# Node MLP on one NeuronCore: edge means transposed in two stacked copies of 64 rows, and their product with the first layer's edge weights made from rounded parts

## What is computed

```
sums   = segment_sum(edge_attr, src)              # 100000 x 64 -> 6250 x 64
counts = segment_sum(ones, src)
edge_attr_agg = sums / max(counts, 1)             # the edge means
combined = concat([layernorm(x), edge_attr_agg, u[batch]], axis=1)   # 256 + 64 + 128 columns
h = relu(combined @ W1 + b1)                      # 512 hidden values
x = x + (h @ W2 + b2)                             # back to 256
```

## Time and profile before

| | us |
|---|---|
| median of 3 runs | 3084.15 (3078.67 to 3087.76) |
| the profiled execution, its own time | 3059.02 |
| span of its instructions | 3056.9 |
| the node MLP, from the last bucket sum to the last T1 | about 1298 to 1484 |
| PE busy in the whole span | 2239.9 (73%) |
| DVE busy | 1911.5 (63%) |
| POOL busy | 2051.8 (67%) |

### The profile page before, as it was taken

The page is one execution under the profiler, slowest core; times in us unless marked ns, Lnnn a source line. Parts: engine busy times, 40 slices in busy tenths (PEclk is TensorE's granted clock), DMA queues, the critical chain, the costliest instruction groups (busy, mean ns, idle before and its releaser), DMA issues.

```text
span 3056.9 us, 49337 instructions
## 1 busy us (share of the span) xinstructions
PE 2239.9 (73%) x14353; PEld 2057.8 (67%) x14354; DVE 1911.5 (63%) x2802; ACT 931.3 (30%) x2542; POOL 2051.8 (67%) x1683
## 2 busy tenths in 40 slices
PE   0000037768999978899699994878888777899897
PEld 0000026658888878877599994766667667899897
DVE  8879986733333222256487767965654555599897
ACT  0000002220111110023466662444544422355453
POOL 5777877777777777201166664787877831588886
PEclk9999998885555555589899997998988885799999
DMA  6543245454444434122112124777777765022231
GB/s 207 152 123 95 77 114 150 144 159 129 126 113 114 119 96 131 60 68 75 41 41 60 50 61 142 196 192 187 197 194 186 195 203 126 25 82 72 64 92 33
DMA packets 342896, 358.31 MB, mean 117 GB/s; under 512 B 210796, under 2 KB 250076, under 8 KB 342513
## 3 DMA queue, kind: packets, MB, share of 16 engines
q1 hardware_dynamic: 210925, 196.63, 22.6%
q0 software_dynamic: 105984, 93.52, 13.5%
q10 hardware_dynamic: 25853, 66.46, 7.0%
HBM read 234.79 MB, written 122.74 MB: 117 GB/s over the span
## 4 chain that ended last, share of the span: by engine, by line
PE 44%; POOL 23%; issue 13%; DVE 13%; DMA 5%; SPq 2%; ACT 1%; DVEq 0%; POOLq 0%; ACTq 0%
POOL sorted L1042 17%; PE ps L2011 13%; POOL mid L1118 5%; PE ps L2060 3%; PE ps L2160 3%; PE ps L2179 2%; PE ps L2038 2%; PE ps L2115 2%; PE ps L2117 2%; PE ps L2116 2%; PE ps L2137 1%; PE ps L2138 1%; PE ps L2136 1%; DVE hT L1650 1%; PE ps L2170 1%
## 5 line engine op out<-in xcount | busy, mean ns | idle before, releaser
L2011 PE MATMUL ps<-big 128*128 128x65 f32 x2380 | 528.1, 420 | 86.7 <-issue 52.5
L2011 PEld LDWEIGHTS ps<-big 128*128 128x128 f32 x2380 | 514.1, 332 | 102.0 <-issue 100.9
L1118 POOL DMA_INDIRECT mid<-h_rows,idx_a x400 | 484.4, 1211 | 131.9 <-issue 115.4
L1415 DVE TENSOR_TENSOR big<-ps,big 128x1792 f32<-128x1792 f32 x85 | 171.6, 2020 | 204.9 <-PE ps L2011 163.3
L1042 POOL DMA_INDIRECT sorted<-yb,idx_a x200 | 239.3, 1196 | 83.9 <-issue 60.0
L1051 POOL TENSOR_TENSOR rstd<-var,neg_half 125x2 f32<-125x2 f32 (+1 forms) x75 | 64.2, 856 | 326.3 <-DVE var L1470 326.1
L1042 POOL DMA_INDIRECT sorted<-xh,idx_b x200 | 237.4, 1187 | 61.0 <-issue 60.3
L1042 POOL DMA_INDIRECT sorted<-mid,idx_b x200 | 237.3, 1187 | 60.9 <-issue 60.3
L1042 POOL DMA_INDIRECT sorted<-wk,idx_a x200 | 237.3, 1187 | 61.0 <-issue 60.3
L2160 PE MATMUL ps<-mid 125*128 125x96 f32 x1600 | 219.8, 300 | 72.2 <-issue 25.1
L2160 PEld LDWEIGHTS ps<-mid 125*128 125x128 f32 x1600 | 211.2, 213 | 84.5 <-issue 57.4
(11 more groups left out here) (336 smaller groups left out, 6307.5 us busy)
## 6 DMA issues: line engine op xcount, KB each, us to landing
h_in_r<-h_parts SPq DMA_DIRECT2D x245, 256.0 KB, 4.4
big<-sorted ACTq DMA_DIRECT2D x85, 469.0 KB, 4.1
sorted<-hT SPq DMA_DIRECT2D x73, 469.0 KB, 7.3
mid<-in_L_ffn_w SPq DMA_DIRECT2D x16, 1024.0 KB
hid_x<-hT ACTq DMA_DIRECT2D x25, 500.0 KB, 4.1
mid<-hid_x SPq DMA_DIRECT2D x25, 500.0 KB
h_parts<-h_part_r SPq DMA_DIRECT2D x25, 480.0 KB
mid<-h_rows,idx_a POOLq DMA_INDIRECT x400
```

Source lines behind the costliest of these rows:

```text
L1118: nc.gpsimd.indirect_dma_start(mg4[:, s, i, :], None, h_rows, bass.IndirectOffsetOnAxis(idx4[:, s, i:i + 1], 0)).then_inc(s_gk[s], 16)
L1415: v.tensor_tensor(node_hot[:, s % 2], lo_near.unsqueeze(1).to_broadcast([BR, GA, BR]), rows2[:, s, :, CW:CW + 1].to_broadcast([BR, GA, BR] ...
L2011: i_ = mm(banks[:, bass.ds(o_, CW)], node_hot[:, s % 2, i, :], rows2[:, s, i, 0:CW], start=False, stop=True, skip_group_check=True)
```

## The change

`agg` becomes `agg2`, two copies of the 64 columns side by side per node, in `big` instead of `mid`: DVE writes the means to the first, ACT copies them to the second, bank by bank. A transpose of such a tile gives 128 rows, the means twice. ACT rounds all 128 rows into `aT`; DVE (`aT_lo`) replaces the lower 64 rows by the rest, exact minus rounded. `aT` then holds high over low parts. The weights are loaded twice too, one copy over the other, and rounded into `wA1e_hi` (128 rows); `wA1e_lo` (64 rows) is the rest of the weights. `hidden` makes each block of 128 hidden values from two products of rounded parts: all 128 rows with `wA1e_hi`, and the upper 64 with `wA1e_lo`. On PE, `means_T(g + 2)` now stands ahead of the second layer; on ACT, `aT_copy(g + 2)` ahead of the relu.

```diff
@@ tiles
-        agg = mid[0:BR, 0:TB * DE].rearrange("p (t d) -> p t d", t=TB)
+        agg2 = big[0:BR, 6256:6256 + 2 * TB * DE].rearrange("p (t c d) -> p t c d", t=TB, c=2)
+        agg = big[0:BR, 6256:6256 + 2 * TB * DE].rearrange("p (t q) -> p t q", t=TB)
+        aT = over("aT", "ends", KEPT, [128, 2, N])
+        wA1e_hi = over("wA1e_hi", "hT", 12 * N, [128, HID0])
+        wA1e_lo = over("wA1e_lo", "mid", 9392, [128, HID0])
+        BANKS = (6, 0, 1, 2, 3, 4, 5)
@@ SP
-                    sp.dma_start(wA1e, w1[D:D + DE, :]).then_inc(s_wA, 16)
+                    for h in range(2):
+                        sp.dma_start(wA1e[h * DE:(h + 1) * DE, :], w1[D:D + DE, :]).then_inc(s_wA, 16)
@@ ACT
-                act.activation(aT[:, s], ps[0:DE, 6, s * N:(s + 1) * N], ACT.Copy).then_inc(s_aTe, 1)
+                act.activation(aT[:, s], ps[:, 6, s * N:(s + 1) * N], ACT.Copy).then_inc(s_aTe, 1)
...
+                if not (fixed and g >= G - 2):
+                    aT_copy(g + 2, s)
                 if not (fixed and g == G - 1):
                     hidden(g + 1, 1 - s)
-                if not (fixed and g >= G - 2):
-                    aT_copy(g + 2, s)
...
-            aT_copy(0, 0)
+            act.wait_ge(s_wA, 80)
+            act.activation(wA1e_hi[:, :], wA1e, ACT.Copy)
+            for j, k in enumerate(BANKS):
+                act.wait_ge(s_a0, j + 1)
+                b = slice(k * PB, (k + 1) * PB)
+                act.activation(agg2[:, b, 1, :], agg2[:, b, 0, :], ACT.Copy).then_inc(s_a1, 1)
+                if j == 3:
+                    aT_copy(0, 0)
             aT_copy(1, 1)
@@ DVE
-            for k in range(7):
-                i_ = v.tensor_tensor(agg[:, k * PB:(k + 1) * PB, :], sums[:, k, :, 0:DE], inv7[:, k, :].unsqueeze(2).to_broadcast([BR, PB, DE]), ALU.mult)
-            i_.then_inc(s_a0, 1)
+            dve.wait_ge(s_kept, 48)
+            for k in BANKS:
+                v.tensor_tensor(agg2[:, k * PB:(k + 1) * PB, 0, :], sums[:, k, :, 0:DE], inv7[:, k, :].unsqueeze(2).to_broadcast([BR, PB, DE]), ALU.mult).then_inc(s_a0, 1)
...
+            def aT_lo(g, s):
+                dve.wait_ge(s_aTe, g + 1)
+                v.tensor_tensor(aT[DE:128, s], ps[DE:128, 6, s * N:(s + 1) * N], aT[DE:128, s].bitcast(f32), ALU.subtract).then_inc(s_aTlo, 1)
...
                     add_hidden(g + 1, 1 - s)
+                if not (fixed and g >= G - 2):
+                    aT_lo(g + 2, s)
                 if not (fixed and g == 0):
                     ln1_rows(g - 1, 1 - s)
...
+            dve.wait_ge(s_aTe, 1)
+            v.tensor_tensor(wA1e_lo[0:DE, :], wA1e[0:DE, :], wA1e_hi[0:DE, :].bitcast(f32), ALU.subtract)
+            aT_lo(0, 0)
+            aT_lo(1, 1)
@@ PE
                 if g == 0:
-                    pe.wait_ge(s_a0, 1)
+                    pe.wait_ge(s_a1, A1 + 2)
                     pe.wait_ge(s_hx, 4 * G)
                 else:
-                    pe.wait_ge(s_aTe, g)
+                    if g == 1:
+                        pe.wait_ge(s_a1, A1 + 7)
+                    pe.wait_ge(s_aTlo, g)
...
-                    i_ = mm(ps[0:DE, 6, at:at + k], agg[:, b, :], ident[:, q:q + k], start=True, stop=True)
+                    i_ = mm(ps[:, 6, at:at + k], agg[:, b], ident[:, q:q + k], start=True, stop=True)
...
-                        i_ = mm(ps[:, 2 + j, m % 2 * N:(m % 2 + 1) * N], wA1e[:, m * 128:(m + 1) * 128], aT[:, s, :], start=True, stop=True)
+                        o_, f = ps[:, 2 + j, m % 2 * N:(m % 2 + 1) * N], slice(m * 128, (m + 1) * 128)
+                        mm(o_, wA1e_hi[:, f], aT[:, s, :], start=True, stop=False)
+                        i_ = mm(o_, wA1e_lo[0:DE, f], aT[0:DE, s, :], start=False, stop=True)
...
                     hidden(g + 1, 1 - s)
+                if not (fixed and g >= G - 2):
+                    means_T(g + 2, s)
...
-                if not (fixed and g >= G - 2):
-                    means_T(g + 2, s)
```

More of the change, by code:

```diff
@@ L167, in build @@
         not_dst = ends[0:P, 2 * ET:KEPT]
-        aT = ends[0:DE, KEPT:KEPT + 2 * N].rearrange("p (s n) -> p s n", s=2)
         idx_a = sb("idx_a", [P, 2, EB], u32)
@@ L288, in build @@
         assert o <= 5850
-        wA1e = mid[0:DE, 5850:5850 + HID0]
+        wA1e = mid[:, 5850:5850 + HID0]
         wA2 = mid[:, 6362:6362 + 4 * D].rearrange("p (c d) -> p c d", c=4)
@@ L407, in build @@
         s_hx, s_hxw, s_hxin = sem("x_hidden_in_sbuf"), sem("x_hidden_written"), [sem(f"x_hidden_back{i}") for i in range(2)]
-        s_a0, s_aT, s_aTe = sem("edge_means_set"), sem("edge_means_T_in_psum"), sem("edge_means_T_in_sbuf")
+        s_a0, s_aT, s_aTe = sem("edge_means_set"), sem("edge_means_T_in_psum"), sem("edge_means_T_hi")
+        s_aTlo = sem("edge_means_T_lo")
         s_h1, s_hadd, s_h1e = sem("edge_hidden_in_psum"), sem("hidden_added"), sem("hidden_in_sbuf")
@@ L437, in build @@
         s_xn, s_y5, s_base, s_sc = sem("slot_rows_normalised"), sem("results_set"), sem("x3_written"), [sem(f"results_scattered{i}") for i in range(2)]
+        s_a1, A1 = s_bAset, 1
         s_dsel2, DSEL2 = s_aT, G
@@ L1948, in _ @@
             mm(ps[0:1, 4, 16:17], met[:, :], ones[:, 0:1], start=True, stop=True).then_inc(s_schp, 1)
-            pe.wait_ge(s_wA, 64)
+            pe.wait_ge(s_wA, 80)
             pe.wait_ge(s_cst, 160)
@@ L2026, in means_T @@
                     k = min(P, BR - q)
-                    i_ = mm(ps[0:DE, 6, at:at + k], agg[:, b, :], ident[:, q:q + k], start=True, stop=True)
+                    i_ = mm(ps[:, 6, at:at + k], agg[:, b], ident[:, q:q + k], start=True, stop=True)
                     if k < P:
-                        i_ = mm(ps[0:DE, 6, at + k:at + P], agg[:, b + 1, :], ident[:, 0:P - k], start=True, stop=True)
+                        i_ = mm(ps[:, 6, at + k:at + P], agg[:, b + 1], ident[:, 0:P - k], start=True, stop=True)
                 i_.then_inc(s_aT, 1)
             def hidden(g, s):
-                pe.wait_ge(s_aTe, g + 1)
+                pe.wait_ge(s_aTlo, g + 1)
                 for j in range(2):
```

## The result

The changed kernel is slower: 3104.36 us median of 4 runs (3101.08 to 3107.47) against 3081.41 (3075.61 to 3087.76) for the kernel before, a ratio of 1.0071 with a 95% interval of 1.0053 to 1.0089. I had forecast 3072 and given "slower" a chance of 0.04.

A forecast was written before the change was run, and what follows sets the result against it. PE alone was taken to bound the node MLP's turns. Hidden -17.1, means_T +9.5 and the start -1.9 made -9.5 us; an earlier clock rise, 3.0 more, made -12.5, from 3084.15 to 3072, range 3063 to 3079.

The forecast's parts named there:

- Hidden, per turn: PE's hidden products in the node MLP: 1.14 us for 1.88, 0.74 less per turn, 17.1 us over 23 turns.
- means_T: PE's transposes of the means: 128-column weight loads make them 1.11 us, 0.43 more per turn, 9.5 us lost over 22.
- Second layer and T1: PE's other work in each node MLP turn: unchanged at 3.66 and 0.58 us.
- Start of the stage: Node MLP start and turn 0 at the low clock: turn 1 begins 1.8 to 1.9 us sooner.
- The clock: PE's clock in the node MLP: rises near 1310.5, 6 us sooner, after 128-row rounded products, saving 3.0 us more.
- My own case: The whole kernel with the early clock rise: -12.5 us, 3072, own range 3068 to 3075, chance 0.50.
- The last rival: Clock falls back in the node MLP: about 6.5 us per turn at 0.50, three such turns give 3079; chance 0.04.
- DVE: DVE in each node MLP turn: aT_lo adds 0.40 us, need 5.5 of 6.49, so it stays hidden.
- Ahead of the stage: Before the node MLP, beside POOL's row stores: the second weight load costs nothing, at most 1 us.

The follow-up runs named there:

- e2: The changed kernel with both products of hidden over the upper 64 rows only, leaving out the low part of the means: 3062.71 us, 0.9936 of the kernel before.
- e1: The changed kernel with hidden's second product over all 128 rows, the lower 64 rows of wA1e_lo zero: 3058.16 us, 0.9923 of the kernel before.
- e3: The changed kernel with the low product first in every second block of hidden, halving the row changes: 3074.32 us, 0.9978 of the kernel before.
- e7: The kernel before with hidden's float32 products over 128 rows, the lower 64 of both operands zero: 3048.10 us, 0.9974 of the kernel before.
- e8: The kernel before with one of three products of the first mixture of experts' hidden layer over 64 rows instead of 128: 3372.11 us (one run).
- e6: The changed kernel with means_T behind the second layer and aT_copy behind relu again, aT_lo left in place: 3200.36 us, 1.0487 of the kernel before.
- e5: The kernel of e1 with aT_lo behind ln1_rows on DVE instead of ahead of it: 3027.14 us, 0.9909 of the kernel before.
- e4: The kernel before, unchanged, run again for its trace: 3080.49 us (one run).

## Why the prediction was wrong

The step that failed is one sentence of "Hidden, per turn": "Half of the products here have 64 rows; before, a 64-row record (1.88 / 8 = 0.235) cost as much as a 128-row one (3.66 / 16 = 0.229), so I give them nothing." It is true of 64-row products that follow each other (e2: 1.13 us for eight) and false of the order in which the change puts them. Weights of 64 and of 128 rows alternate, and each load then waits for the product ahead. Hidden measured 2.46 us against 1.14. Over 23 turns that is 30 us, which turns my -9.5 into +21. That this is so near the measured +20.6 is in part luck, since four other terms were off and cancel: the spells of low clock (+8.4) and the start (+5.0) against second layer and T1 (-8.6) and means_T (-4). e1 to e3 show the step by row count and order, with the same number of products throughout.

A hint stood in the trace before, and I read over it. The last record of hidden (0.30 us to the next start) and the first of the second layer (0.32) each took about 0.1 more than the records between (0.21 and 0.22). My two means, 0.235 and 0.229, each held half of a change and so looked alike. e7 shows it: 0.09 and 0.10 us went with the padding.

The Trainium skill has a rule that I did not bring in. "TensorEngine Tiling (Array Packing)", under "Key Properties", says that changing the tiling mode, not just the tile, drains the TensorE. That fits e1, e2, e3, e7 and e8, if a plain product over 64 rows counts as another mode than one over 128, which the page does not say. It gives no figure; the runs put it at 0.19 us per change in the changed kernel at the high clock (0.31 against 0.118) and 0.29 at the low one (e8).

The other steps:

- **means_T**: 0.91 to 0.98 us against my 1.11, on the mean 0.25 more than before at the same place and not 0.43. That the wide loads cost something holds; the term was too large. e1's 0.84 has no change of rows ahead of it, so without that change it is 0.15 more than before.
- **Second layer and T1**, which I held at 3.66 and 0.58, fell to 3.50 and 0.35. I had not costed what stands beside each; 0.39 per turn comes back in the new order. A part is seen in rows: before, the last two records of the second layer take 0.52 us up to means_T, whose weights have 64 columns (1324.80 to 1325.32); in e6, where the weights behind them have 128 columns, three take 0.64 (1327.32 to 1327.96). So a change of columns seems to cost too. No experiment was made for it.
- **Start of the stage**: means_T(0) began 2.65 us after `inv` instead of 4.7 (1325.59 and 1302.97), as worked out. Hidden(0) and hidden(1) then took 8.1 us (1330.86 to 1338.96) against my 3.8 and the 6.96 before. The second layer of turn 0 came 18.0 us after `inv` instead of 15.0.
- **The clock**: I expected an earlier rise and got a later one. My own case rested on it. From the start of hidden(0) to the rise it took 5.0, 8.3 and 8.4 us with 128 rows throughout (e7, e1, e5), 9.2 with 64-row rounded products (e2), 9.7, 10.3 and 11.3 in three traces of the old stage (e8, before, e4), and 10.1, 12.2 and 13.5 where the heights alternate (e3, e6, the changed kernel). The order fits my guess that 128-row work brings the rise sooner, but one and the same stage varies by 1.7 us, so it is not shown. The last rival named the clock falling back and priced a spell by the turn; the spells came, five of them, but short ones, 8.4 us in all and not 6.5 each. The sum in that rival was wrong as well: from -12.5 us, three such turns give +7.0, 3091 and not 3079. The spells are absent in e1, e2 and e3. In the ten traces, one per run, a spell of low clock in the turns of the node MLP stands only in the changed kernel, in which every load of hidden waits, and (with gaps between the products) in e6; e3, with half of the changes, has none. What made the clock fall stays open.
- **DVE**: right for the changed kernel, where PE never waits for it in the turns. aT_lo took 0.42 us (0.40 expected). It came into play once PE's turn fell to 5.7 us (e1), where I had put DVE's need at 5.5; with the 0.42 behind ln1_rows (e5) most of the wait went.
- **Ahead of the stage**: nothing, as said. The second weight transfer and the wait on the stored ends cost nothing that can be seen: the bucket sums end at 1322.1 in e4, at 1322.9 in the changed kernel and at 1322.2 to 1323.1 in e1 to e3, which have both.

With the rows mended the rest of the sum is close: e1 moves the stage by -21.6 us. The sum for it is -9.5, less 0.39 x 22 = 8.6 given back by second layer and T1, less 0.12 x 23 + 0.27 x 22 = 8.7 by which e1's hidden (1.02) and means_T (0.84) beat my 1.14 and 1.11, which makes -26.8; the mean turn of 5.99 stands 0.26 above PE's work of 5.73, 5.7 over 22 turns, the wait for DVE: -21.1.

## What to carry to other kernels

Before splitting a product into parts, write down the row count of every weight load in the order in which PE gets them. If it changes between 64 and 128 from one to the next, pad the short one with zero rows, or put products of one height side by side; here a padded product took the 0.115 us of a full one (e1). Other heights were not tried, except that T1's 125 rows beside 128 show no such cost: in e1, T1 and hidden together take 1.37 us, for four records at 0.106 and eight at 0.115. Where a stage is bound by PE, a first record that costs more than its followers deserves a cause of its own before the change is priced.

## What was unexpected about the hardware

- Adding 64 zero rows to half of the products made the kernel 42 us faster in the stage (208.1 to 165.9).
- Each change between 64 and 128 rows cost 0.19 us at the high clock and 0.29 at the low one. With two products of one height side by side it was paid once for both, 0.43 us per pair (e3).
- With every product of hidden waiting for its weights, the granted clock dropped from 1.00 to 0.50 for 3 to 4 us at a time, though PE was busy throughout by the profile; in e8 its mean was 0.70 over 300 us. Why it fell is open.
- The same program ended its bucket sums at 1298 us on one chip (e8) and at 1322 on the other (e4), a difference larger than what the change is worth.
